# Router weights by DMA into all partitions, scaled on GpSimd, in place of a broadcast matmul

## The reference

```
h = einsum('bcij,ce->bije', x summed over 16x16 patches, channel_weights)   # 196 tokens x 192
h = h + attn(layernorm(h))           # the first 64 tokens attend to the other 132; a projection
h = h + ffn(layernorm(h))            # mixture of 8 experts (2 per token) and a shared one
```

```
scores = sigmoid(x2 @ gate_weight.T); the best 2 experts of the best 2 groups are taken
h = silu(x2 @ w1[e].T) * (x2 @ w3[e].T)          # 128 values per token and expert
y = sum over e of w[t, e] * (h @ w2[e].T)        # plus the shared expert, which has no weight
```

## Time and profile before

| | us |
|---|---|
| median of 3 runs | 1875.4 (1872.0 to 1878.65) |
| the profiled execution's own time | 1880.6 |
| its span, first to last instruction | 1878.9 |
| busy: PE / DVE / ACT / POOL | 1634.6 / 1239.9 / 905.8 / 657.5 |
| mean granted TensorE clock | 0.935 of full speed |

### The profile page before, as it was taken

One profiled execution on the slowest core, in us unless ns is written; L12 is line 12 of the kernel. 1 busy time (PEld: TensorE's weight loads), 2 busy tenths in 40 slices (PEclk: granted clock), 3 DMA queues, 4 the chain that ended last, 5 costly groups with the idle time before them and its releaser, 6 DMA issues.

```text
span 1878.9 us, 31672 instructions
## 1 busy us (share of the span) xinstructions
PE 1634.6 (87%) x9665; PEld 1260.1 (67%) x9798; DVE 1239.9 (66%) x2344; ACT 905.8 (48%) x2999; POOL 657.5 (35%) x739
## 2 busy tenths in 40 slices
PE   1714639999999989998999989998999999999998
PEld 1203528866787667766787667766787678877876
DVE  6855567577666687578566677578666764566365
ACT  2324433656356654656355654656365643443132
POOL 5334326334443435334443335334534332000000
PEclk9955659989999899989999899999999999999999
DMA  8896755546554465555455455556554530000000
GB/s 304 315 352 239 289 219 196 205 165 222 205 204 182 172 222 216 180 200 207 175 205 204 168 215 204 182 198 223 195 205 174 210 131 10 10 18 18 9 19 26
DMA packets 55455, 333.14 MB, mean 177 GB/s; under 512 B 4237, under 2 KB 33666, under 8 KB 33774
## 3 DMA queue, kind: packets, MB, share of 16 engines
q1 hardware_dynamic: 55062, 330.51, 47.6%
q10 hardware_dynamic: 216, 0.50, 0.1%
HBM read 311.10 MB, written 19.27 MB: 176 GB/s over the span
## 4 chain that ended last, share of the span: by engine, by line
PE 69%; DVE 14%; issue 7%; DMA 6%; ACT 2%; POOL 1%; SPq 1%; DVEq 0%; ACTq 0%; another core or an unknown queue 0%; POOLq 0%
PE bank L1370 25%; PE bank L1218 19%; DMA xt<-in_x 6%; PE bank L1392 6%; PE bank L1397 3%; DVE pooled L770 2%; PE bank L1285 2%; DVE ffn L1123 2%; PE bank L1313 2%; DVE ffn L1133 2%; PE bank L1325 2%; PE bank L1274 1%; PE bank L1280 1%; PE bank L1297 1%; PE bank L1290 1%
## 5 line engine op out<-in xcount | busy, mean ns | idle before, releaser
L1370 PE MATMUL bank<-W2T,ffn 128*128 128x192 f32 (+1 forms) x3600 | 692.8, 331 | 0.0
L1370 PEld LDWEIGHTS bank<-W2T,ffn 128*128 128x128 f32 (+1 forms) x3600 | 599.7, 190 | 54.3 <-issue 6.5
L1123 DVE TENSOR_TENSOR ffn<-bank,ffn 128x512 f32<-128x512 f32 (+1 forms) x448 | 278.3, 621 | 367.7 <-PE bank L1218 161.7
L560 POOL TENSOR_TENSOR kh_sum<-xt 128x768 f32<-128x768 f32 (+2 forms) x168 | 249.1, 1483 | 738.0 <-DMA xt<-in_x 730.1
L732 ACT ACTIVATE ffn<-bank 128x512 f32<-128x512 f32 (+1 forms) x504 | 274.1, 547 | 396.0 <-PE bank L1392 211.0
L630 ACT ACTIVATE xt<-xt 128x256 f32<-128x256 f32 x776 | 312.5, 411 | 110.1 <-DMA xt<-in_x 110.1
L1133 DVE TENSOR_TENSOR ffn<-bank,ffn 128x512 f32<-128x512 f32 (+1 forms) x448 | 279.5, 624 | 40.6 <-DVE ffn L1123 33.1
L1392 PE MATMUL bank<-tokT,Wx 126*128 126x512 bf16 (+1 forms) x720 | 250.9, 353 | 25.2 <-DVE ffn L1133 12.6
L770 DVE TENSOR_REDUCE pooled<-xt 128x1 f32<-128x256 f32 (+2 forms) x168 | 233.4, 1389 | 38.9 <-DMA xt<-in_x 38.0
L555 POOL TENSOR_TENSOR kh_sum<-kh_sum 128x384 f32<-128x384 f32 (+2 forms) x336 | 230.2, 685 | 26.4
L1218 PE MATMUL bank<-x0h,WT0h 128*128 128x512 f32 x288 | 154.6, 537 | 3.0 <-issue 2.3
(11 more groups left out here) (253 smaller groups left out, 2161.8 us busy)
## 6 DMA issues: line engine op xcount, KB each, us to landing
xt<-in_x SPq DMA_DIRECT2D x168, 1792.0 KB, 7.3
out<-stage SPq DMA_DIRECT2D x192, 96.0 KB
ffn<-in_L_ffn_w SPq DMA_DIRECT2D x2, 768.0 KB
attw<-in_L_ffn_w SPq DMA_DIRECT2D x1, 512.0 KB
Wx<-tokT ACTq DMA_DIRECT2D x9, 54.2 KB
out<-stage SPq DMA_DIRECT2D x8, 48.0 KB
attw<-in_L_ffn_w SPq DMA_DIRECT2D x1, 256.0 KB
ffn<-in_L_ffn_sw SPq DMA_DIRECT2D x2, 96.0 KB
```

The costliest lines, as they stand in the source:

```text
L560: nc.gpsimd.tensor_tensor(out=kh, in0=src[:, 0:8, :], in1=src[:, 8:16, :], op=ALU.add).then_inc(pool_read, 1)
L1123: v.tensor_tensor(out=gated[p][:, 0:n], in0=h_ps(step, 1)[:, 0:n], in1=silu[p][:, 0:n], op=ALU.mult).then_inc(gated_done, 1)
L1370: last = mm(o, h[step % HR][:, 128 * t:128 * t + m], W2T[:, e, :], start=(e == 0 and query and t % 2 == 0), stop=(e == NE), skip_group_che ...
```

## The change

- The matmul L1397, its bank, `sel`, `cwT` and the three-part bf16 split are gone. h1 and h3 now have two banks each.
- The "C" items transpose the f32 weights of the 8 experts straight from `gt`, ACT copies them to small staging areas, SP stores them to a DRAM tensor `cw_rows` (7 DMAs per group, up to 16 KB each).
- For each of the 56 weighted steps of a group SP loads one row of 512 (or 64) values into all 128 partitions (`partition_broadcast`), 256 KB or 32 KB of SBUF each. The loads go through SP's queue, five steps ahead (`CW_AHEAD`), into a ring of seven buffers (`CW_RING`).
- POOL multiplies silu by the landed row in place (`scale`), and DVE makes one product per step, h3 times the scaled row. It waits for POOL (`scaled`) in place of ACT.
- From tile 19 of group 1 on POOL sums no tiles. DVE takes 9 columns (5 in the tile's step, 4 in the next), ACT 5 (3 and 2).
- Each power on POOL is cut in two halves; gates have 36 instructions instead of 40; "C" is two steps earlier.

```diff
-SHARE = {"dve": (0, 7), "act": (7, 9), "pool": (9, NP)}
-SHARE_K = {"dve": (0, 1), "act": (1, 8), "pool": (8, NP)}
+SHARE = {"dve": [(0, 5), (5, 9)], "act": [(9, 12), (12, NP)], "pool": None}
+CW_RING = 7
+CW_AHEAD = 5
@@ SP
+            def cw_rows_out(g, step):
+                for kind, i in items_at(step):
+                    if kind == "C":
+                        n = 512 if i < 6 else 64
+                        sp.wait_ge(aux_act, g.at(BYACT[-1], BYACT[R[("C", i)]]))
+                        sp.dma_start(cw_rows[g.par, :, 512 * i:512 * i + n], cw_stage[i][:, 0:n])\
+                          .then_inc(cw_out[1 if i else 0], 16)
+            def cw_load(g, step):
...
+                def slot_free(use):
+                    back = use - CW_RING
+                    wait(sp, h_done, g.at(STEPS, back // NE * EX + back % NE + 1))
...
+                sp.dma_start(cwb[slot][:, 0:n], cw_rows[g.par, e, at:at + n].partition_broadcast(128))\
+                  .then_inc(cw_landed[slot], 16)
+            def cw_ahead(g, step, left):
+                if left:
+                    cw_rows_out(g.plus(1), step)
+                if step + CW_AHEAD < STEPS:
+                    if g.off >= 0:
+                        cw_load(g, step + CW_AHEAD)
+                elif left:
+                    cw_load(g.plus(1), step + CW_AHEAD - STEPS)
             def ffn_dma(g, left):
                     for gt_, t in tiles_at(g, step, left):
                         load_after(gt_, t)
+                    cw_ahead(g, step, left)
                     if e == 3 and c > 0:
                         store(g, c - 1)
@@ POOL
+            def scale(g, step):
...
+                pool.wait_ge(cw_landed[slot], g.at(16 * CW_USES // CW_RING, 16 * (use // CW_RING + 1)))
+                pool.wait_ge(silu_done, g.at(STEPS, step + 1))
+                nc.gpsimd.tensor_tensor(out=cwb[slot][:, 0:n], in0=silu[(g.par + step) % 2][:, 0:n],
+                                        in1=cwb[slot][:, 0:n], op=ALU.mult).then_inc(scaled, 1)
             def ffn_pool(g, left):
                 for step in range(STEPS):
+                    scale(g, step)
                     step_pool(g, step, left)
@@ DVE
-                        v.tensor_tensor(out=gated[p][:, 0:n], in0=h_ps(step, 1)[:, 0:n], in1=silu[p][:, 0:n],
-                                        op=ALU.mult).then_inc(gated_done, 1)
...
-                        v.tensor_tensor(out=h[step % HR][:, 0:n], in0=cw_ps[:, 0:n], in1=gated[p][:, 0:n],
-                                        op=ALU.mult).then_inc(h_done, 1)
+                    v.tensor_tensor(out=h[step % HR][:, 0:n], in0=h_ps(g, step, 1)[:, 0:n],
+                                    in1=(silu[p] if e == NE else cwb[(c * NE + e) % CW_RING])[:, 0:n],
+                                    op=ALU.mult).then_inc(h_done, 1)
@@ PE
-                    wait(pe, gated_done, g.at(STEPS, step - 1))
+                    wait(pe, h_done, g.at(STEPS, step - 1))
...
-                        mm(cw_ps[:, 0:n], sel[:, e, :], cwT[:, at:at + n], start=True, stop=True).then_inc(cw_ready, 1)
```

More of the change, by code:

```diff
@@ L115 @@
     43: [("keyG", 1), ("G", 0)],
-    59: [("C", 0), ("C", 1)],
-    60: [("C", 2), ("C", 6)],
-    61: [("C", 3), ("C", 4), ("C", 5)],
+    57: [("C", 0), ("C", 1)],
+    58: [("C", 2), ("C", 6)],
+    59: [("C", 3), ("C", 4), ("C", 5)],
 }
 A_FIRST = 2
-GATES = 40
-for _s in range(14):
+GATES = 36
+for _s in range(12):
     PLAN[45 + _s] = [("gate", n) for n in range(3 * _s, min(GATES, 3 * _s + 3))] + PLAN.get(45 + _s, [])
@@ L148, in share, with pool_sums @@
 def share(g, t):
[L150 to L153, removed]
+    return SHARE0 if pool_sums(g, t) else SHARE
+def pool_sums(g, t):
+    return g.k is None and g.off * TILES + t < POOL_TILES
 def tiles_at(g, step, groups_left=2):
@@ L443, in load @@
             def load(g, t):
-                for s in (dve_summed, act_summed, pool_read):
+                for s in (dve_summed, act_summed):
                     wait(sp, s, g.at(TILES, t - SLOTS + 1))
+                if pool_sums(g, t - SLOTS):
+                    wait(sp, pool_read, g.at(TILES, t - SLOTS + 1))
                 slot = g.slot(t)
@@ L490, in _ @@
                     load_after(gt_, t)
+                cw_ahead(G(None, -1), step, 1)
             ffn_dma(G(None, 0), 2)
@@ L535, in _ @@
                                          pattern=[[CH, 8]], channel_multiplier=-1))
-            link(nc.gpsimd.memset(sel[:, :, :], 0.0))
-            for s in range(SPL):
-                link(nc.gpsimd.affine_select(out=sel[:, :, :], in_=sel[:, :, :], compare_op=ALU.not_equal, fill=1.0,
-                                             base=-NE * s, pattern=[[-1, NE], [0, 128]], channel_multiplier=1))
             for i in range(NE):
@@ L712, in step_act @@
             def step_act(g, step, left):
[L714 to L720 removed]
+                for back in (1, 0):
+                    for gt_, t in tiles_at(g, step - back, left):
+                        parts = share(gt_, t)["act"]
+                        if back < len(parts):
+                            act_tile(gt_, t, *parts[back], back == len(parts) - 1)
                 if left:
@@ L729, in ffn_act @@
                     act.wait_ge(h1_ready, g.at(STEPS, step + 1))
-                    wait(act, gated_done, g.at(STEPS, step - 1))
+                    wait(act, h_done, g.at(STEPS, step - 1))
                     p = (g.par + step) % 2
-                    nc.scalar.activation(silu[p][:, 0:n], h_ps(step, 0)[:, 0:n], ACT.Silu).then_inc(silu_done, 1)
+                    nc.scalar.activation(silu[p][:, 0:n], h_ps(g, step, 0)[:, 0:n], ACT.Silu).then_inc(silu_done, 1)
                     if e == 1 and c > 2:
@@ L1090, in gates, with step_dve @@
                     ins.then_inc(dve_link, 1)
-            def step_dve(g, step, left, skip=0):
+            def step_dve(g, step, left):
                 if left:
-                    for kind, i in items_at(step)[skip:]:
+                    for kind, i in items_at(step):
                         item(g.plus(1), "S_max" if kind == "S" else kind, i)
-                for gt_, t in tiles_at(g, step, left):
-                    dve_sums(gt_, t)
+                for back in (1, 0):
+                    for gt_, t in tiles_at(g, step - back, left):
+                        if back < len(share(gt_, t)["dve"]):
+                            dve_sums(gt_, t, back)
             def evacuate(g, c):
```

174 lines of the change are left out of this document (88 added, 86 removed).

## The result

The changed kernel takes 1955.1 us (median of 4 runs, 1947.5 to 1957.0) against 1877.0 of the kernel before on the same chip: 1.041 times as long, 95% interval 1.0385 to 1.0435. The forecast was 1845, faster than before. The kernel is 78 us slower instead, and 52 us above the top of the widest range given (1903).

The account below looks back on a forecast made before the run. PE was taken as the bound, DVE in gate steps with tiles. -88 matmul, +18 gates, +17 powers, +19 tiles, +4 transposes gave -30 us, from 1875.4 to 1845; range 1815 to 1870, with rivals 1787 to 1903.

Parts of the forecast that it names:

- The matmul that goes: PE without the wide router matmuls: 11 us a group saved, 88 over eight groups.
- tiles at 10 a group: Tile cost in groups 0 to 5 if rows land in time: -35 us in place of +19.
- the transposes: 25 C transposes a group in f32 instead of bf16: half a microsecond each group, 4 us in all.
- The new chain of a step: From h1's start through silu, POOL's and DVE's products to h: 3.2 us, fitting within 3.48.
- the rival of a slow POOL: Rival: POOL's product slower than 1.27 us; at 1.8, 25 us are lost, giving 1870; chance 0.12.
- DVE, the port and the powers: Gate steps gain nothing because of the shared port, 18 us; scaling waits behind POOL's powers, 17 us; groups 0 to 6.
- The first powers: POOL's halved powers around steps 4 to 8 delay the next scale: 2.5 us a group, groups 0 to 6.
- The loads in SP's queue: Rows behind tile loads land late in some key steps: 8.5 us a group; tiles cost 19 a group, +19 in all.
- Late rows as the bound: Rival: late rows in steps 22 to 58 cost 28 us a group, deciding from 24; 1899 us, chance 0.23.
- the 10.5 for the blocks of ACT and DVE: Part of the old 15.9 us tile cost a group kept for remaining tile blocks on ACT and DVE.
- Loads in time: Rival: rows land before the chain needs them, tiles cost 10 us a group; 1791 us, chance 0.2.
- The check list: Signs to show: group 7's step pace, POOL's 1.27 us product, where rows wait (2 to 4 us), and group times.

Follow-up runs that it names:

- no_scale: Changed kernel without router-row loads and without GpSimd's product; VectorE multiplies h3 by silu, expert weights left out: 1753.5 us.
- no_rows: Changed kernel without the router-row loads; GpSimd multiplies silu by itself, expert weights left out: 1818.1 us.
- ring8_first: Changed kernel with each row issued ahead of the step's tile in SP's queue, ring of eight, rows up to seven steps ahead: 1877.9 us.
- act_late: Changed kernel with row loads in ScalarE's queue and a group's first six rows asked for in steps 61, 62 and 0: 1878.5 us.
- late_t44: act_late with a group's last five tiles in steps 44, 48, 52, 56 and 59 instead of 46, 49, 52, 55 and 58: 1858.7 us.
- act_late_c59: act_late with the C transposes back in steps 59 to 61, as in the kernel before: 1935.6 us.

## Why the prediction was wrong

**The matmul that goes** was right as far as the runs can tell. By the prediction's terms the kernel without loads and without the product would lie at -88 for the matmul, -35 for tiles at 10 a group and +4 for the transposes: -119. `no_scale` measured -123. Its group 7, with neither items nor tiles, takes 145.6 us against 157.1, 11.5 less where 11 were forecast.

**The new chain of a step** was right in its size: in group 7 silus follow each other by 1.73 (1925.61, 1927.34, 1929.08) and query steps by 3.64; POOL's product:

```profile
L654 POOL TENSOR_TENSOR ffn<-ffn 128x512 f32<-128x512 f32 (+1 forms) x448 | 512.8, 1149 | 1020.1 <-ACT ffn L803 653.2
L629 POOL TENSOR_TENSOR stat<-stat,mhalf 98x16 f32<-98x16 f32 x32 | 94.4, 2953 | 36.0 <-DVE stat L978 22.8
```

The 384 wide ones take 1.29 us in the mean (1.27 forecast), so the rival of a slow POOL falls. A half power takes 2.95 (2.8 forecast). The Trainium skill (GPSIMD Engine Reference, Elementwise side-by-side cycle accounting) gave an estimated 1.1 before fixed costs; the trace agrees.

**DVE, the port and the powers** were counted at 18 + 17 = 35 us; the product costs 65. The first powers were right, 2.1 us a group against 2.5. The power of x2 (L580, 1.65 us in the profile before, among none of the rows that I chose) was put at nothing: it is one more long POOL instruction with the product behind it, in the shortest steps of all, and steps 27 to 35 pay 3.2 us a group. That PE's clock falls in such waits was named in a rival and had no price. The gates did suffer about as forecast, but in full only with the rows: in group 6 the gate steps take 3.0 us more in the changed kernel than in `no_scale` (2.6 counted), and 1.2 more in `no_rows`. So gate work is not most of the 65 us.

**The loads in SP's queue is the step that failed.** It read the mechanism of a late row rightly, priced it too low, and put all else that loads cost at nothing. Landing 8 us after the tile's issue: 7.3 measured (1507.37 to 1514.72). The row of step 34 late by 3.5: 3.7. But the list was short and the others cheap: the rows of 51, 54, 57 and 60 at 2 us every second time, 46 at 1, query steps safe, 8.5 us a group in sum. Group 5 has eleven late rows and 29.9 us. The paragraph's own working gives more than it charged: 13 us from silu to the scale, less 8.2 and 0.6, are 4.2 us for a row of the gate steps, of which "about 2 late every second time" was kept, although the chain's slack was 0.3 by its own count; 4.9, 4.4 and 2.1 were measured. Three things were missing besides. First the loop: "a late row also puts off the next tile" stood there, with no price, while the tile's issue came 7.9 us after its step's silu (1499.51 to 1507.37) and not one step and 3.9. Second the stores: the earlier trace rows showed SP held for 6.54 us by the third store behind a tile, and nothing was charged to rows that stand behind them, as that of step 36 (3.0 late in group 5). Group 7 took 151.7 us instead of the 146.5 of `no_rows`, nearly all of it in steps 37 and 38, behind the row of step 36, which had been issued behind four stores and was 2.5 us late. Third, the shortest steps (27 to 35) were checked for one row only.

The prediction charged the loads with 54 us (19 in place of -35); they cost 137. Of these, 77 went away with the lateness (`ring8_first`, `act_late`), against 54 charged. The other 60 it put at nothing: a kernel whose rows land in time was to have no cost from them (-35, tiles at 10 a group). Group 6 shows such costs: it was to take 187 us and took 199.7 (189.2 without the loads) with one late row, that of step 0, 1.8 us late. Of the 10.5 us, 4.2 are in steps 36 to 38 and 1.5 in step 22, where the granted clock was at half (1726.4 to 1740.0 and 1695.7 to 1699.1; in `no_rows` for 3.4 us of the whole group), and 1.2 are in step 55, with two gate instructions of 1.13 and 1.30 us beside POOL's product. What made the clock fall there, and how the 60 us divide over all groups, stays open; 20 of them went away in `late_t44`, by the steps of the tiles alone. With the 30 of the product and 4 of the first sum in the other sense these are 109 of the 110 us between 1845 and 1955.

**The rivals.** Late rows as the bound was the nearest one, at 1899. Its sum left something out: its 28 us a group are late rows alone, and the 10.5 for the blocks of ACT and DVE, kept in the forecast, are missing. With them it would have been 1962, near the 1955 measured, but partly by luck, as it has too little for the product. Its condition, tiles at more than 24 us a group, was a wrong test: group 6 served as the zero line and was itself longer, so tiles are 220.8 - 199.7 = 21.1 us by that count. Its price of 2 us at a key tile is below the 3.0 to 5.0 of six rows in group 5. "Loads in time" is best seen in `ring8_first` and `act_late`, at 1878, and even with loads that cost nothing (`no_rows`) it would be 1818, not 1791.

**The check list** held in part: the pace of group 7, POOL's product, few waits in query steps, waits after step 30 and from 46 to 58. It did not hold for groups 0 to 5 (220.8 us, 205 forecast), group 6 (199.7, 187), group 7 (5.4 shorter, 10) and the size of the waits (up to 7.4 us, 2 to 4), and rows were late at 18 to 27 and 36 too. Its last line said that I was wrong if waits stood in most key steps. In group 5 there were ten of them in 40 weighted key steps, and that was enough.

## What to carry to other kernels

A small load behind a large one in the same queue waited here for the large one's landing (7.5 us instead of 3.4); ask what stands ahead of it, stores too, and issue it ahead of the large one and earlier, or from another engine. Take the lateness away in one run and the loads in another: the two differed by 60 us here. When a late load delays the work that frees the buffer for the next large load, price the loop and not the single lateness, by walking the shortest steps one by one. A helper instruction put into a chain must be checked against every long instruction of that engine, not only those the change touches.

## What the hardware showed

- A row written to 128 partitions (256 KB) landed in a median of 3.4 us in group 7, with no tiles about, 7.5 in SP's queue among tiles, 5.0 in ScalarE's (`act_late`). Half the partitions: 4.6. A tile's landing was 7.3 us before, 7.4 with the rows in the same queue, and 7.9 to 8.1 with them in a second one.
- 16 KB to DRAM behind a 1792 KB load in the same queue (`act_late_c59`): 8.9 us until it counted as done.
- POOL's 128x512 product took 1.29 us with two different inputs and 1.05 with the same one twice.
- A gate addition on DVE (L1139) took 0.837 us in the changed kernel and 0.357 in `no_rows` (medians). The Trainium skill (SBUF — State Buffer, Who interferes with whom) says that a DVE instruction with two SBUF inputs and a GpSimd one that reads SBUF exclude each other. The traces agree, in `no_rows` too. A gate instruction with two inputs that begins within a product ends just behind it (DVE and POOL in the changed kernel, then in `no_rows`):

```profile
1779.25 1.30 DVE L1131 TENSOR_TENSOR gt<-gt,gs 128x200 f32<-128x200 f32 x1
1779.06 1.27 POOL L654 TENSOR_TENSOR ffn<-ffn 128x512 f32<-128x512 f32 x1 [0.47 <-ACT ffn L803]
```

```profile
1639.48 0.77 DVE L1100 TENSOR_TENSOR gt<-gt,gs 128x200 f32<-128x200 f32 x1
1638.99 1.04 POOL L639 TENSOR_TENSOR ffn<-ffn 128x512 f32<-128x512 f32 x1 [0.80 <-ACT ffn L788]
```

Of 80 gate instructions of this kind (`TENSOR_TENSOR`, 128x200, two inputs) 24 met work of POOL in the changed kernel and 5 in `no_rows`. So the medians differ because the two met less often there, not because POOL reads one tile twice. A `tensor_scalar` of the gates with one input (L1064) took up to 1.13 us beside a product in `no_rows` and 0.25 in `no_scale`; the same section of the Trainium skill counts such instructions in, in their two-port modes, which the prediction left out.
